# Attention in units of four heads: half-dimension tiles, scores over 32-row groups, new order of turns and evacuations

## The chip, the cores and the metric

The kernel runs on one core of a Trainium2 chip. The metric is the device time of one execution in microseconds (us). Names used below: PE is TensorE (PEld its weight loads), DVE is VectorE, ACT is ScalarE, POOL is GpSimd, SP is SyncE, which issues the DMAs.

## The reference

The whole reference is a chain of six residual blocks on x of shape (8, 256, 128) (in float32): a graph of small attentions, the attention below, the graph again, a mixture of experts, a Mamba block with an FFT branch, and the mixture again. The change touches only the second block:

```python
xn = (x - mu) / sqrt(var + 1e-5) * ln_gamma + ln_beta        # on _layernorm(x)
q, k, v = split(xn @ w_qkv)                                   # 16 heads of 64, 8 batches of 256 tokens
rotate(t) = concat([t1 * cos - t2 * sin, t2 * cos + t1 * sin])   # t1, t2: halves (32) of a head's 64 dimensions
scores = einsum('bhid,bhjd->bhij', rotate(q), rotate(k)) * 64 ** -0.5
out = einsum('bhij,bhjd->bhid', softmax(scores), v)
x = x + out.reshape(b, n, 1024) @ w_out + b_out
```

## The kernel before

The program is a row of phases with a barrier of all engines between them. In the attention phase (`attn_phase`) the unit of work is one pair of heads of one batch: 8 batches times 8 pairs are 64 units. All operands are float32; a float32 matmul appears in the trace as two MATMUL and two LDWEIGHTS instructions, a transpose as one of each.

`attn_schedule` runs one step per unit with four units in flight: f is projected, m (one behind) gets scores and exponentials, t (two behind) is normalized, turned and multiplied with v, u (three behind) goes through the output projection. Each engine has its own queue in program order, and counters (semaphores) tie them.

- TensorE: four projections of 256 columns (L796: q and k in a plain form, and q and k with the halves of each head swapped), v (L805), scores (L815: four matmuls of 256 columns; the keys lie in `km` with zeros in the other head's rows, so that each contracts over all 128 rows), eight transposes of the probabilities (L825), the output projection (L833, accumulated over the eight pairs of a batch in one bank), the context (L842, two column groups of 64).
- VectorE: reciprocal of the row sums (L856), normalization of the probabilities (L859, four instructions), the products with cos and sin (L868, one 512-column instruction for plain and one for swapped), row maximum (L873, one instruction over 1024 columns), its scaling (L875), the sums for k (L883), and once per batch the addition to x (L888).
- GpSimd: the sum for q (L911), a copy of the batch's tokens (L907).
- ScalarE: evacuation of v (L921), of the transposes (L926), four exponentials with row sums (L930), evacuation of the context (L935).

Seven banks of PSUM are in use: `plain`, `swapped`, two for scores, two for transposes (`tp`), one for v and context (`vc`), and `op`. The phase begins with five DMAs (L783, L784), all of which TensorE waits for.

Of the kernel before, what the change touches and what calls it, by code (L numbers as in the profile page):

```python
# [715 lines left out]
PAIRS = HA // 2  # L716
# [3 lines left out]
class Unit:  # L720


    def __init__(self, b, p):
        self.b, self.p, self.n = b, p, b * PAIRS + p


def attn_schedule(engine, step):

    def units(b, p, first=False):
        out = []  # L730
        for back in range(4):
            if p >= back:
                out.append(Unit(b, p - back))
            else:
                out.append(None if first else Unit(b - 1, p - back + PAIRS))
        return out

    for p in range(PAIRS):
        step(*units(0, p, first=True))
    with engine.Fori(1, B) as b:  # L740
        for p in range(PAIRS):
            step(*units(b, p))
    for late in range(1, 4):
        step(*([None] * late + [Unit(B - 1, PAIRS - 1 - i) for i in range(4 - late)]))


def attn_phase(k):

    nc, d = k.nc, k.d
    with ExitStack() as ctx:  # L750
        wqk = k.sb("at_wqk", [P, 4, HA * DA], ctx)
        wv = k.sb("at_wv", [P, HA * DA], ctx)
        wo = k.sb("at_wo", [P, PAIRS, D], ctx)
        rope = k.sb("at_rope", [P, 2, N], ctx)
        bo = k.sb("at_bo", [P, D], ctx)
        xb = k.sb("at_xb", [P, N], ctx)
        rot = k.sb("at_rot", [P, 2, 2, N], ctx)
        q = k.sb("at_q", [P, 2, N], ctx)
        km = k.sb("at_km", [P, 2, 2, N], ctx)
        v = k.sb("at_v", [P, VBUFS, 2, 2, DA], ctx)  # L760
        mx = k.sb("at_mx", [P, 2, 4], ctx)
        nmx = k.sb("at_nmx", [P, 2, 4], ctx)
        rsum = k.sb("at_rsum", [P, 2, 4], ctx)
        rinv = k.sb("at_rinv", [P, 2, 4], ctx)
        pr = k.sb("at_pr", [P, 2, 4, N], ctx)
        pt = k.sb("at_pt", [P, 2, 2, N], ctx)
        cx = k.sb("at_cx", [P, N], ctx)
        plain = k.psum("at_plain", [P, 2, N], ctx)
        swapped = k.psum("at_swapped", [P, 2, N], ctx)
        sc = k.psum("at_sc", [P, 4, N], ctx)  # L770
        tp = k.psum("at_tp", [P, 2, 2, N], ctx)
        vc = k.psum("at_vc", [P, 2, N], ctx)
        op = k.psum("at_op", [P, 512], ctx)
        names = ["loaded", "zeroed", "bias", "xb_sb", "proj_ps", "v_ps", "v_sb", "rot_sb", "q_sb", "km_sb", "sc_ps", "mx_sb", "nmx_sb",
# [3 lines left out]
        loads = [(wqk, "wqk"), (wv, "wv1"), (wo, "wout"), (rope, "rope")]  # L778

# [6 lines left out]
        @block.tensor  # L786
        def _(pe):
            def step(f, m, t, u):
                if f:

                    if not isinstance(f.n, int) or f.n:
                        pe.wait_ge(s["rot_sb"], f.n)
                    xs = k.xT[:, bass.ds(f.b * N, N)] if not isinstance(f.b, int) else k.xT[:, f.b * N:(f.b + 1) * N]
                    for i in range(4):
                        bank = plain if i < 2 else swapped
                        last = nc.tensor.matmul(bank[:, i % 2, :], wqk[:, i, f.p * P:(f.p + 1) * P], xs, start=True, stop=True)  # L796
                    last.then_inc(s["proj_ps"], 1)
                if f:
                    pe.wait_ge(s["xb_sb"], f.b + 1)
                    if u:  # L800
                        pe.wait_ge(s["cx_sb"], u.n + 1)
                    elif f.n:
                        pe.wait_ge(s["v_sb"], f.n)
                    for half in range(2):
                        last = nc.tensor.matmul(vc[:, 0, half * P:(half + 1) * P], xb[:, half * P:(half + 1) * P],  # L805
                                                wv[:, f.p * P:(f.p + 1) * P], start=True, stop=True)
                    last.then_inc(s["v_ps"], 1)
                if m:
                    pe.wait_ge(s["q_sb"], m.n + 1)
                    pe.wait_ge(s["km_sb"], m.n + 1)  # L810
                    if not isinstance(m.n, int) or m.n:
                        pe.wait_ge(s["pr_sb"], m.n)
                    for h in range(2):
                        for qh in range(2):
                            last = nc.tensor.matmul(sc[:, 2 * h + qh, :], q[:, m.p % 2, qh * P:(qh + 1) * P],  # L815
                                                    km[:, m.p % 2, h, :], start=True, stop=True)
                    last.then_inc(s["sc_ps"], 1)
                if t:
                    pe.wait_ge(s["pn_sb"], t.n + 1)
                    if not isinstance(t.n, int) or t.n:  # L820
                        pe.wait_ge(s["pt_sb"], 2 * t.n)
                    for h in range(2):
                        for qh in range(2):
                            for kh in range(2):
                                last = nc.tensor.transpose(tp[:, h, kh, qh * P:(qh + 1) * P],  # L825
                                                           pr[:, t.p % 2, 2 * h + qh, kh * P:(kh + 1) * P], k.ident[:, :])
                        last.then_inc(s["tp_ps"], 1)
                if u:
                    pe.wait_ge(s["cx_sb"], u.n + 1)
                    if u.p == 0 and (not isinstance(u.b, int) or u.b):  # L830
                        pe.wait_ge(s["x_sb"], u.b)
                    for half in range(2):
                        last = nc.tensor.matmul(op[:, half * P:(half + 1) * P], cx[:, half * P:(half + 1) * P], wo[:, u.p, :],  # L833
                                                start=u.p == 0 and half == 0, stop=u.p == PAIRS - 1, skip_group_check=True)
                    last.then_inc(s["op_ps"], 1)
                if t:
                    pe.wait_ge(s["pt_sb"], 2 * t.n + 2)
                    if f:
                        pe.wait_ge(s["v_sb"], f.n + 1)
                    for kh in range(2):  # L840
                        for h in range(2):
                            last = nc.tensor.matmul(vc[h * DA:(h + 1) * DA, 1, :], v[:, t.p % VBUFS, kh, h, :],  # L842
                                                    pt[:, h, kh, :], start=kh == 0, stop=kh == 1, tile_position=(0, h * DA))
                    last.then_inc(s["cx_ps"], 1)

            pe.wait_ge(s["loaded"], 16 * (len(loads) + 1))
            pe.wait_ge(s["zeroed"], 1)
            attn_schedule(pe, step)

        @block.vector  # L850
        def _(dve):
            def step(f, m, t, u):
                if t:

                    dve.wait_ge(s["pr_sb"], t.n + 1)
                    nc.vector.reciprocal(rinv[:, t.p % 2, :], rsum[:, t.p % 2, :]).then_inc(s["rinv_sb"], 1)  # L856
                    dve.wait_ge(s["rinv_sb"], t.n + 1)
                    for i in range(4):
                        last = nc.vector.tensor_scalar(pr[:, t.p % 2, i, :], pr[:, t.p % 2, i, :], rinv[:, t.p % 2, i:i + 1],  # L859
                                                       None, ALU.mult)  # L860
                    last.then_inc(s["pn_sb"], 1)
                if f:
                    dve.wait_ge(s["proj_ps"], f.n + 1)
                    if not isinstance(f.n, int) or f.n:
                        dve.wait_ge(s["q_sb"], f.n)
                        dve.wait_ge(s["km_sb"], f.n)
                    for i, bank in enumerate((plain, swapped)):
                        last = nc.vector.tensor_tensor(rot[:, i, :, :], bank[:, :, :],  # L868
                                                       rope[:, i:i + 1, :].broadcast_to([P, 2, N]), ALU.mult)
                    last.then_inc(s["rot_sb"], 1)  # L870
                if m:
                    dve.wait_ge(s["sc_ps"], m.n + 1)
                    nc.vector.tensor_reduce(mx[:, m.p % 2, :], sc[:, :, :], AX.X, ALU.max).then_inc(s["mx_sb"], 1)  # L873
                    dve.wait_ge(s["mx_sb"], m.n + 1)
                    nc.vector.tensor_scalar(nmx[:, m.p % 2, :], mx[:, m.p % 2, :], -(float(DA) ** -0.5), None, ALU.mult)\  # L875
                        .then_inc(s["nmx_sb"], 1)
                if f:
                    dve.wait_ge(s["rot_sb"], f.n + 1)
                    if not isinstance(f.n, int) or f.n >= 2:
                        dve.wait_ge(s["sc_ps"], f.n - 1)  # L880
# [972 lines left out]
```

## Time and profile before

| | us |
|---|---|
| median of three runs | 2776.11 (2773.88 to 2781.83) |
| the profiled execution's own time | 2771.16 |
| its span | 2769.3 |
| TensorE busy in the span | 2219.1 (80%) |
| VectorE, ScalarE, GpSimd busy | 1956.6, 1330.9, 812.3 |
| attention: first DMA issue, first matmul, end of the last addition to x | 608.3, 619.6, 1069.3 |

Busy time of a matmul includes its way through the array, so that consecutive ones overlap in the records; the pace is read from the starts of successive groups. "PEclk" is the granted clock of TensorE as a share of 2.4 GHz. A row of the order of time gives start, duration, engine, line, operation, output and inputs, and in brackets the idle time of that engine before it and who ended it.

### The profile page before, as it was taken

Reading aid. Unit: us, or ns where it says so; the run is one execution under the profiler, and the core shown is the slowest. Engines: PE = TensorE matmul, PEld = TensorE weight load, DVE = VectorE, ACT = ScalarE, POOL = GpSimd, SP = SyncE. Lnnn points to the kernel's source line nnn. Section 1 sums busy time; section 2 is a strip of 40 time slices with the busy share of each in tenths; the row PEclk is TensorE's granted clock in tenths of the full one; section 3 lists DMA queues with packets and bytes.
Section 4 is the critical chain, followed back from the end, with each engine's and each line's share of the span. In section 5 each row is a group of like instructions: output and inputs, shape, how many; then the busy total and the mean of one; then the engine's idle time right before and its main releaser. Section 6 shows DMA issues by size and latency. Waiting matters only on the chain. (4 is left out here: it accounts for less than half of the span.)

```text
span 2769.3 us, 41693 instructions
## 1 busy us (share of the span) xinstructions
PE 2219.1 (80%) x14388; PEld 1629.2 (59%) x14388; DVE 1956.6 (71%) x3310; ACT 1330.9 (48%) x2702; POOL 812.3 (29%) x1144
## 2 busy tenths in 40 slices
PE   2799999919999994799999946486877878878858
PEld 2466666617777773466666624274665655756634
DVE  4566666566666665566666554489899898998964
ACT  0466666615555552466666613345445445364422
POOL 0544444201111110544444202023323223233323
PEclk7899999959999997799999968698989989999969
DMA  1555555310000000555555300200000000000000
GB/s 62 144 132 136 134 138 133 79 52 1 1 0 0 0 0 0 145 133 136 135 137 132 78 14 12 116 0 0 1 1 1 1 0 0 0 0 1 1 12 15
DMA packets 147427, 144.31 MB, mean 52 GB/s; under 512 B 14401, under 2 KB 107201, under 8 KB 146497
## 3 DMA queue, kind: packets, MB, share of 16 engines
q1 hardware_dynamic: 147264, 142.23, 19.3%
q8 instruction: 92, 1.51, 0.2%
q14 instruction: 71, 0.57, 0.1%
HBM read 93.95 MB, written 38.80 MB: 48 GB/s over the span
## 5 line engine op out<-in xcount | busy, mean ns | idle before, releaser
L559 DVE TENSOR_REDUCE sb_f_mx<-ps_f_s 128x2 f32<-128x512 f32 x768 | 505.3, 688 | 315.8 <-PE ps_f_s L347 315.0
L500 ACT ACTIVATE sb_f_pt<-ps_f_t 128x1024 f32<-128x1024 f32 x384 | 391.7, 1021 | 90.3 <-PE ps_f_t L360 90.1
L1707 POOL TENSOR_TENSOR sb_mb_h<-sb_mb_h 128x1024 f32<-128x1024 f32 x64 | 157.7, 2464 | 656.5 <-DVE sb_mb_h L1601 656.5
L347 PE MATMUL ps_f_s<-sb_f_stack 96*128 96x256 bf16 x1536 | 287.4, 279 | 39.3 <-DMA sb_f_stack<-f_scr 22.1
L1595 DVE TENSOR_TENSOR_SCAN sb_mb_h<-sb_mb_da,sb_mb_h 128x1024 f32<-128x1024 f32 x128 | 310.5, 2466 | 2.4 <-ACT sb_mb_da L1466 0.3
L1336 PE MATMUL ps_mb_f<-sb_mb_fc,sb_mb_cw 128*128 128x256 f32 x1280 | 308.5, 404 | 0.0
L1336 PEld LDWEIGHTS ps_mb_f<-sb_mb_fc,sb_mb_cw 128*128 128x128 f32 x1280 | 260.2, 206 | 41.4
L1466 ACT ACTIVATE sb_mb_da<-sb_mb_dl,sb_mb_an 128x255 f32<-128x255 f32 x512 | 211.4, 496 | 70.2 <-DVE sb_mb_h L1595 65.7
L360 PE MATMUL ps_f_t<-sb_f_stack 128*128 128x256 bf16 x1536 | 233.0, 274 | 2.9 <-DMA sb_f_stack<-sb_f_mrow 2.8
L347 PEld LDWEIGHTS ps_f_s<-sb_f_stack 96*128 96x128 bf16 x1536 | 141.1, 99 | 91.2 <-DVE sb_f_mx L559 45.3
L619 POOL CAST sb_f_parts<-sb_f_qf 128x512 bf16<-128x512 f32 x96 | 58.5, 609 | 447.9 <-ACT sb_f_qf L527 447.9
L414 PE MATMUL ps_f_a<-sb_f_pt,sb_f_v 128*32 128x256 f32 x3072 | 185.7, 382 | 0.0
L360 PEld LDWEIGHTS ps_f_t<-sb_f_stack 128*128 128x128 bf16 x1536 | 141.1, 97 | 61.2 <-issue 38.7
L911 POOL TENSOR_TENSOR sb_at_q<-sb_at_rot 128x256 f32<-128x256 f32 x64 | 46.6, 728 | 394.1 <-DVE sb_at_rot L868 394.1
L1367 PE MATMUL ps_mb_c<-sb_mb_bc,sb_mb_sel 128*128 128x256 bf16 x256 | 46.1, 311 | 142.8 <-DVE sb_mb_h L1601 142.7
L1601 DVE TENSOR_TENSOR sb_mb_h<-sb_mb_h,ps_mb_c 128x1024 f32<-128x1024 f32 x128 | 150.6, 1218 | 2.2
L1587 DVE TENSOR_TENSOR sb_mb_h<-ps_mb_b,sb_mb_dx 128x1024 f32<-128x1024 f32 x128 | 150.3, 1216 | 0.7
L511 ACT ACTIVATE sb_f_cs<-ps_f_a 128x512 f32<-128x512 f32 x96 | 57.4, 597 | 186.7 <-PE ps_f_a L414 186.7
L414 PEld LDWEIGHTS ps_f_a<-sb_f_pt,sb_f_v 128*32 128x32 f32 x3072 | 90.1, 109 | 81.0 <-issue 31.6
L926 ACT ACTIVATE sb_at_pt<-ps_at_tp 128x512 f32<-128x512 f32 x128 | 69.6, 595 | 115.9 <-PE ps_at_tp L825 115.9
L815 PE MATMUL ps_at_sc<-sb_at_km,sb_at_q 128*128 128x256 f32 x512 | 121.3, 380 | 2.2 <-ACT sb_at_pr L930 2.2
L132 PE MATMUL ps_n_tp<-sb_ident,sb_n_y 128*128 128x128 f32 x96 | 24.5, 426 | 118.4 <-DVE sb_n_y L124 118.4
(242 smaller groups left out, 4571.7 us busy)
## 6 DMA issues: line engine op xcount, KB each, us to landing
f_scr<-sb_f_parts SPq DMA_DIRECT2D x96, 384.0 KB, 2.7
sb_f_stack<-f_scr SPq DMA_DIRECT2D x192, 192.0 KB, 3.1
sb_f_stack<-f_scr SPq DMA_DIRECT2D x192, 128.0 KB, 3.1
sb_f_stack<-f_scr SPq DMA_DIRECT2D x192, 64.0 KB, 3.4
sb_f_stack<-sb_f_mrow SPq DMA_DIRECT2D x96, 96.0 KB
sb_mb_cw<-in_cw SPq DMA_DIRECT2D x1, 5120.0 KB, 18.5
sb_at_wqk<-in_wqk SPq DMA_DIRECT2D x1, 2048.0 KB, 7.9
sb_m_w<-in_w SPq DMA_DIRECT2D x6, 256.0 KB, 3.2
```

The costliest lines, as they stand in the source:

```text
L347: last = nc.tensor.matmul(s_bank[j % 2][:, h, :], stack[0:ROWS, a.n % STACKS, 0, g * GROUP + pair * 2 + h, half * P:(half + 1) * P], stack ...
L360: last = nc.tensor.matmul(t_bank[i % 2][:, h, :], stack[:, e.n % STACKS, 1, g * GROUP + h, half * P:(half + 1) * P], stack[:, e.n % STACKS ...
L414: last = nc.tensor.matmul(act_bank[h * SLOT:(h + 1) * SLOT, g * N:(g + 1) * N], v[:, u.two, half, g * GROUP + h, :], pt[:, u.two, g, half, ...
L500: nc.scalar.activation(pt[:, e.two, g, half, :, :], t_bank[i % 2][:, :, :], ACT.Exp).then_inc(s["pt_sb"], 1)
L559: nc.vector.tensor_reduce(mx[:, a.two, half, head:head + 2], s_bank[j % 2][:, :, :], AX.X, ALU.max)\
L815: last = nc.tensor.matmul(sc[:, 2 * h + qh, :], q[:, m.p % 2, qh * P:(qh + 1) * P], km[:, m.p % 2, h, :], start=True, stop=True)
L1336: last = nc.tensor.matmul(f_bank[(1 + oc // 2) % 2][:, (oc % 2) * N:(oc % 2 + 1) * N], cw[:, ic, tap, oc * P:(oc + 1) * P], fc[:, ic, tap: ...
L1466: last = nc.scalar.activation(da[:, un % 2, c, i, 1:N], dl[:, m.parity, r, c, 1:N], ACT.Exp, scale=an[:, r, c, n:n + 1])
L1587: last = nc.vector.tensor_tensor(hb[:, c, :, :], b_bank[:, :, :], dx[:, m.parity, r, c:c + 1, :].broadcast_to([P, SG, N]), ALU.mult)
L1595: last = nc.vector.tensor_tensor_scan(flat, da[:, un % 2, c, :, :].rearrange("p i n -> p (i n)"), flat, 0.0, ALU.mult, ALU.add)
L1601: last = nc.vector.tensor_tensor(hb[:, c, :, :], hb[:, c, :, :], c_bank[:, :, :], ALU.mult)
L1707: nc.gpsimd.tensor_tensor(hb[:, :, 0:2, :], hb[:, :, 0:2, :], hb[:, :, 2:4, :], ALU.add)\
```

## The change

The unit becomes four heads of one batch (32 units, 36 steps written out one after another). q and k are projected as half-dimension tiles: four heads times 32 dimensions fill the 128 rows, first halves in one tile and second halves in another, so the swapped projections, `km`, its zeros and the copy `xb` are gone. VectorE multiplies each tile pair with cos and with sin (`rotate`), GpSimd does the two additions (one a subtraction) of q and the two of k. The scores of a head are two accumulated matmuls over its 32 rows, with `tile_position` giving the row group; the four heads write to four banks. Softmax lags two steps behind the projection, the transposes three, the output projection four. The output projection of a unit is written to half of the bank `vc`, and VectorE adds it to x once per unit. Transposes have two banks and come in two portions of two heads; evacuations, exponentials and normalizations are interleaved in halves.

```diff
+QUADS = HA // 4
+UNITS_A = B * QUADS
+SOFT_LAG, TURN_LAG, PROJ_LAG = 2, 3, 4
...
+        sc = [k.psum(f"at_sc{h}", [P, 2, N], ctx) for h in range(4)]
+        tp = [k.psum(f"at_tp{i}", [P, 2, N], ctx) for i in range(2)]
+        proj = k.psum("at_proj", [P, 2, N], ctx)
         vc = k.psum("at_vc", [P, 2, N], ctx)
...
+            def project(f, which):
+                if f.n or which:
+                    pe.wait_ge(s["rope_sb"], 2 * f.n + which)
+                for half in range(2):
+                    last = nc.tensor.matmul(proj[:, half, :], wqk[:, 2 * which + half, f.p, :], k.xT[:, f.b * N:(f.b + 1) * N],
+                                            start=True, stop=True)
+                last.then_inc(s["proj_ps"], 1)
+            def values(f, o):
+                if o:
+                    pe.wait_ge(s["x_sb"], o.n + 1)
...
+            def scores(m):
+                pe.wait_ge(s["rot_sb"], 4 * m.n + 4)
+                if m.n:
+                    pe.wait_ge(s["pr_sb"], 4 * m.n)
+                for qh in range(2):
+                    for half in range(2):
+                        for h in range(4):
+                            rows = slice(h * HALF, (h + 1) * HALF)
+                            last = nc.tensor.matmul(sc[h][:, qh, :], rot[rows, m.two, 0, half, qh * P:(qh + 1) * P],
+                                                    rot[rows, m.two, 1, half, :], start=half == 0, stop=half == 1,
+                                                    tile_position=(h * HALF, 0))
+                last.then_inc(s["sc_ps"], 1)
...
+            def add(o):
+                dve.wait_ge(s["op_ps"], o.n + 1)
...
+                nc.vector.tensor_tensor(xs, xs, vc[:, 0, :].rearrange("p (t d) -> p t d", t=2), ALU.add)\
+                    .then_inc(s["x_sb"], 1)
...
+        @block.gpsimd
...
+            def rotate(f, which):
+                pool.wait_ge(s["rope_sb"], 2 * f.n + which + 1)
...
+                nc.gpsimd.tensor_tensor(rot[:, f.two, which, 0, :], turned[:, which, 0, 0, :], turned[:, which, 1, 1, :],
+                                        ALU.subtract).then_inc(s["rot_sb"], 1)
+                nc.gpsimd.tensor_tensor(rot[:, f.two, which, 1, :], turned[:, which, 0, 1, :], turned[:, which, 1, 0, :],
+                                        ALU.add).then_inc(s["rot_sb"], 1)
```

With f = step, m = step - 2, t = step - 3 and o = step - 4, each engine's calls in a step are, in this order:

- TensorE: `scores(m)`, `turn(t, 0)`, `turn(t, 1)`, `project(f, 0)` (q), `turn(t, 2)`, `turn(t, 3)`, `project_out(o)`, `values(f, o)`, `project(f, 1)` (k), `context(t)`
- VectorE: `row_max(m, 0)`, `row_max(m, 1)`, `rotate(f, 0)`, `invert(m, 0)`, `normalize(m, 0)`, `add(o)`, `rotate(f, 1)`, `invert(m, 1)`, `normalize(m, 1)`
- ScalarE: `evacuate(t, 0)`, `evacuate(t, 1)`, `exponent(m, 0)`, `exponent(m, 1)`, `evacuate(t, 2)`, `evacuate(t, 3)`, v of f, `exponent(m, 2)`, `exponent(m, 3)`, `context(t)`
- GpSimd: `rotate(f, 0)`, `rotate(f, 1)`

The bodies that are not quoted carry the instructions of before at new sizes: `turn` is four transposes of one head, `context` eight matmuls in two column groups, `project_out` four matmuls of 128 columns, `project` and `values` two of 256; VectorE's `rotate` two products of 512 columns, `row_max` two reductions of 512 columns and one scaling, `normalize` four instructions of 256 columns; `evacuate` one copy of 512 columns, `exponent` two exponentials with row sums. `project_out(o)` waits for ScalarE's copy of the context, made in the step before.

## Rows read from the trace of the kernel before

**Rows 1.** Busy time by stretch: length, PE, PEld, DVE, ACT, POOL, clock, DMA.

```profile
608.30:619.60 11.30, 0.00 (x0) 0.00 (x0) 0.91 (x2) 0.00 (x0) 0.40 (x1) 0.55 0.81 307
...
634.20:1060.10 425.90, 402.16 (x2478) 329.61 (x2476) 293.10 (x691) 225.13 (x745) 47.26 (x69) 1.00 0.00 0
```

**Rows 2.** Order of time, one step of attention, with the batch's addition.

```profile
746.23 0.42 DVE L888 TENSOR_TENSOR sb_x<-sb_x,ps_at_op 128x256 f32 x1
...
748.94 1.89 PE L815 MATMUL ps_at_sc<-sb_at_km,sb_at_q 128*128 128x256 f32 x8
...
750.07 0.72 POOL L911 TENSOR_TENSOR sb_at_q<-sb_at_rot 128x256 f32<-128x256 f32 x1 [6.14 <-DVE sb_at_rot L868]
...
750.67 1.04 PE L825 MATMUL ps_at_tp<-sb_ident,sb_at_pr 128*128 128x128 f32 x8
750.87 1.23 DVE L873 TENSOR_REDUCE sb_at_mx<-ps_at_sc 128x4 f32<-128x1024 f32 x1 [0.88 <-PE ps_at_sc L815]
751.31 1.09 ACT L926 ACTIVATE sb_at_pt<-ps_at_tp 128x512 f32<-128x512 f32 x2 [1.78 <-PE ps_at_tp L825]
...
752.13 0.17 DVE L875 TENSOR_SCALAR sb_at_nmx<-sb_at_mx 128x4 f32<-128x4 f32 x1
...
752.34 0.47 ACT L930 ACTIVATE sb_at_pr<-ps_at_sc,sb_at_nmx 128x256 f32<-128x256 f32 x1
...
752.52 1.08 PE L842 MATMUL ps_at_vc<-sb_at_pt,sb_at_v 128*64 128x256 f32 x8 [0.37 <-ACT sb_at_pt L926]
...
753.54 1.13 PE L796 MATMUL ps_at_plain<-sb_xT,sb_at_wqk 128*128 x4
...
754.15 0.40 ACT L935 ACTIVATE sb_at_cx<-ps_at_vc 128x256 f32<-128x256 f32 x1
...
754.30 0.18 DVE L856 RECIPROCAL sb_at_rinv<-sb_at_rsum 128x4 f32<-128x4 f32 x1 [1.24 <-ACT sb_at_pr L930]
754.50 1.03 PE L796 MATMUL ps_at_swapped<-sb_xT,sb_at_wqk 128*128 x4
754.51 1.14 DVE L859 TENSOR_SCALAR sb_at_pr<-sb_at_pr,sb_at_rinv 128x256 f32<-128x256 f32 x4
...
755.37 0.61 PE L805 MATMUL ps_at_vc<-sb_at_wv,sb_at_xb 128*128 128x128 f32 x4
755.57 0.69 DVE L868 TENSOR_TENSOR sb_at_rot<-ps_at_plain,sb_at_rope 128x512 f32<-128x512 f32 x1
...
755.81 1.89 PE L815 MATMUL ps_at_sc<-sb_at_km,sb_at_q 128*128 128x256 f32 x8
...
756.18 0.68 DVE L868 TENSOR_TENSOR sb_at_rot<-ps_at_swapped,sb_at_rope 128x512 f32<-128x512 f32 x1
```

**Rows 3.** Order of time, first graph phase: four column groups, and two reductions.

```profile
301.54 1.93 PE L414 MATMUL ps_f_a<-sb_f_pt,sb_f_v 128*32 128x256 f32 x32
...
303.40 0.61 PE L360 MATMUL ps_f_t<-sb_f_stack 128*128 128x256 bf16 x4
...
306.17 1.28 DVE L559 TENSOR_REDUCE sb_f_mx<-ps_f_s 128x2 f32<-128x512 f32 x2
```

**Rows 4.** Order of time: VectorE beside GpSimd, in attention's first step and in Mamba.

```profile
624.78 1.29 DVE L883 TENSOR_TENSOR sb_at_km<-sb_at_rot 64x256 f32<-64x256 f32 x2
...
624.83 0.96 POOL L911 TENSOR_TENSOR sb_at_q<-sb_at_rot 128x256 f32<-128x256 f32 x1 [14.88 <-DVE sb_at_rot L868]
...
1901.71 1.27 POOL L1710 TENSOR_TENSOR sb_mb_h<-sb_mb_h 128x512 f32<-128x512 f32 x1
1901.89 1.51 DVE L1631 TENSOR_SCALAR sb_mb_vv<-sb_mb_vv,sb_mb_zo 128x256 f32<-128x256 f32 x2
```

**Rows 5.** After idle time of TensorE: one row of time, two stretches as in rows 1.

```profile
1063.48 1.97 PE L825 MATMUL ps_at_tp<-sb_ident,sb_at_pr 128*128 128x128 f32 x8 [2.18 <-DVE sb_at_pr L859]
...
1063.40:1066.80 3.40, 3.32 (x16) 2.90 (x18) 0.03 (x1) 1.20 (x2) 0.00 (x0) 0.51 0.00 0
...
2002.10:2005.50 3.40, 3.40 (x5) 1.33 (x4) 3.37 (x4) 3.05 (x5) 0.69 (x1) 0.51 0.00 0
```

More of the change, by code:

```diff
@@ L715, with __init__, attn_unit @@
 HA, DA = 16, 64
-PAIRS = HA // 2
+QUADS = HA // 4
+HALF = DA // 2
+UNITS_A = B * QUADS
+SOFT_LAG, TURN_LAG, PROJ_LAG = 2, 3, 4
 VBUFS = 4
 class Unit:
[L723 to L744, printed above, removed]
+    def __init__(self, n):
+        self.n = n
+        self.b, self.p = divmod(n, QUADS)
+        self.two = n % 2
+def attn_unit(step, lag):
+    return Unit(step - lag) if 0 <= step - lag < UNITS_A else None
 def attn_phase(k):
@@ L778, in attn_phase @@
         loads = [(wqk, "wqk"), (wv, "wv1"), (wo, "wout"), (rope, "rope")]
+        steps = range(UNITS_A + PROJ_LAG)
+        scale = float(DA) ** -0.5
         @block.sync
@@ L787, in _ @@
         def _(pe):
-            def step(f, m, t, u):
-                if f:
[L791 to L839, printed above, removed]
@@ new lines, in turn @@
+            def turn(t, h):
+                pe.wait_ge(s["pn_sb"], 2 * t.n + h // 2 + 1)
+                if t.n or h >= 2:
+                    pe.wait_ge(s["pt_sb"], 4 * t.n + h - 1)
+                for qh in range(2):
+                    for kh in range(2):
+                        last = nc.tensor.transpose(tp[h % 2][:, kh, qh * P:(qh + 1) * P],
+                                                   pr[:, t.two, 2 * h + qh, kh * P:(kh + 1) * P], k.ident[:, :])
+                last.then_inc(s["tp_ps"], 1)
@@ L840, in step, with context @@
+            def context(t):
+                f = attn_unit(t.n, -TURN_LAG)
+                o = attn_unit(t.n, 1)
+                pe.wait_ge(s["pt_sb"], 4 * t.n + 4)
+                if f:
+                    pe.wait_ge(s["v_sb"], f.n + 1)
+                elif o:
+                    pe.wait_ge(s["x_sb"], o.n + 1)
+                for pair in range(2):
                     for kh in range(2):
                         for h in range(2):
-                            last = nc.tensor.matmul(vc[h * DA:(h + 1) * DA, 1, :], v[:, t.p % VBUFS, kh, h, :],
-                                                    pt[:, h, kh, :], start=kh == 0, stop=kh == 1, tile_position=(0, h * DA))
@@ new lines, in context, with project_out @@
+                last.then_inc(s["cx_ps"], 1)
+            def project_out(o):
+                pe.wait_ge(s["cx_sb"], o.n + 1)
+                for half in range(2):
+                    for pair in range(2):
+                        last = nc.tensor.matmul(vc[:, 0, half * P:(half + 1) * P], cx[:, o.two, pair, half * P:(half + 1) * P],
+                                                wo[:, 2 * o.p + pair, :], start=pair == 0, stop=pair == 1)
+                last.then_inc(s["op_ps"], 1)
+            pe.wait_ge(s["loaded"], 16 * (len(loads) + 1))
@@ new lines, in _ @@
+            for step in steps:
+                f, m = attn_unit(step, 0), attn_unit(step, SOFT_LAG)
+                t, o = attn_unit(step, TURN_LAG), attn_unit(step, PROJ_LAG)
+                if m:
+                    scores(m)
+                if t:
+                    turn(t, 0)
+                    turn(t, 1)
+                if f:
+                    project(f, 0)
+                if t:
+                    turn(t, 2)
+                    turn(t, 3)
+                if o:
+                    project_out(o)
+                if f:
+                    values(f, o)
+                    project(f, 1)
+                if t:
+                    context(t)
@@ L850, in _ @@
         @block.vector
         def _(dve):
[L852 to L871, printed above, removed]
-                    dve.wait_ge(s["sc_ps"], m.n + 1)
[L873 to L880, printed above, removed]
-                    for h in range(2):
-                        rows = slice(h * DA, (h + 1) * DA)
-                        last = nc.vector.tensor_tensor(km[rows, f.p % 2, h, :], rot[rows, 0, 1, :], rot[rows, 1, 1, :], ALU.add)
-                    last.then_inc(s["km_sb"], 1)
-                if u and u.p == PAIRS - 1:
-                    dve.wait_ge(s["op_ps"], u.n + 1)
-                    xs = k.x[:, bass.ds(u.b * 2, 2), :] if not isinstance(u.b, int) else k.x[:, 2 * u.b:2 * u.b + 2, :]
-                    nc.vector.tensor_tensor(xs, xs, op[:, 0:N].rearrange("p (t d) -> p t d", t=2), ALU.add)\
-                        .then_inc(s["x_sb"], 1)
@@ new lines, in row_max @@
+            def row_max(m, pair):
+                if pair == 0:
+                    dve.wait_ge(s["sc_ps"], m.n + 1)
+                for h in (2 * pair, 2 * pair + 1):
+                    last = nc.vector.tensor_reduce(mx[:, m.two, 2 * h:2 * h + 2], sc[h][:, :, :], AX.X, ALU.max)
+                last.then_inc(s["mx_sb"], 1)
+                dve.wait_ge(s["mx_sb"], 2 * m.n + pair + 1)
+                nc.vector.tensor_scalar(nmx[:, m.two, 4 * pair:4 * pair + 4], mx[:, m.two, 4 * pair:4 * pair + 4], -scale,
+                                        None, ALU.mult).then_inc(s["nmx_sb"], 1)
@@ new lines, in invert, with normalize @@
+            def invert(m, pair):
+                dve.wait_ge(s["pr_sb"], 4 * m.n + 2 * pair + 2)
+                nc.vector.reciprocal(rinv[:, m.two, 4 * pair:4 * pair + 4], rsum[:, m.two, 4 * pair:4 * pair + 4])\
+                    .then_inc(s["rinv_sb"], 1)
+            def normalize(m, pair):
+                dve.wait_ge(s["rinv_sb"], 2 * m.n + pair + 1)
+                for i in range(4 * pair, 4 * pair + 4):
+                    last = nc.vector.tensor_scalar(pr[:, m.two, i, :], pr[:, m.two, i, :], rinv[:, m.two, i:i + 1],
+                                                   None, ALU.mult)
+                last.then_inc(s["pn_sb"], 1)
@@ L896, in _ @@
             dve.wait_ge(s["bias"], 1)
-            attn_schedule(dve, step)
+            for step in steps:
+                f, m, o = attn_unit(step, 0), attn_unit(step, SOFT_LAG), attn_unit(step, PROJ_LAG)
+                if m:
+                    row_max(m, 0)
+                    row_max(m, 1)
+                if f:
+                    rotate(f, 0)
+                if m:
+                    invert(m, 0)
+                    normalize(m, 0)
+                if o:
+                    add(o)
+                if f:
+                    rotate(f, 1)
+                if m:
+                    invert(m, 1)
+                    normalize(m, 1)
@@ L916, in _, with evacuate @@
+            for step in steps:
+                f = attn_unit(step, 0)
+                if f:
+                    rotate(f, 0)
+                    rotate(f, 1)
         @block.scalar
         def _(act):
-            def step(f, m, t, u):
+            def evacuate(t, h):
+                act.wait_ge(s["tp_ps"], 4 * t.n + h + 1)
+                if t.n and h == 0:
+                    act.wait_ge(s["cx_ps"], t.n)
+                nc.scalar.activation(pt[:, h, :, :], tp[h % 2][:, :, :], ACT.Copy).then_inc(s["pt_sb"], 1)
@@ new lines, in context, with exponent @@
+            def context(o):
+                act.wait_ge(s["cx_ps"], o.n + 1)
+                if o.n >= 2:
+                    act.wait_ge(s["op_ps"], o.n - 1)
+                nc.scalar.activation(cx[:, o.two, :, :], vc[:, :, :], ACT.Copy).then_inc(s["cx_sb"], 1)
+            def exponent(m, h):
+                act.wait_ge(s["nmx_sb"], 2 * m.n + h // 2 + 1)
+                if m.n >= 2 and h == 0:
+                    act.wait_ge(s["tp_ps"], 4 * (m.n - 1))
+                for i in (2 * h, 2 * h + 1):
+                    last = nc.scalar.activation(pr[:, m.two, i, :], sc[h][:, i % 2, :], ACT.Exp, scale=scale,
+                                                bias=nmx[:, m.two, i:i + 1], accum_out=rsum[:, m.two, i:i + 1])
+                last.then_inc(s["pr_sb"], 1)
@@ L940 @@
+                if m:
+                    exponent(m, 2)
+                    exponent(m, 3)
+                if t:
+                    context(t)
 EXPERTS, HID = 8, 64
```

113 lines of the change are left out of this document (55 added, 58 removed).

## Prediction, made before the changed kernel was run

> **What bounds the kernel now.** I read the busy time by stretch first, since the change touches one phase, and then the order of time of one step. From 634 to 1060 us TensorE is busy for 402 of 425.9 us at a granted clock of 1.00, VectorE for 293, ScalarE for 225, GpSimd for 47 [rows 1]: attention is bound by TensorE. A step takes 755.81 - 748.94 = 6.87 us [rows 2], in which TensorE has one stall of 0.37 us (the context waits for ScalarE's copy of the transposes). Four heads therefore cost 13.74 us now, and the phase 449.7 us from its first matmul to its last addition. Ahead of it stand 11.3 us in which the five DMAs run at 307 GB/s and TensorE does nothing [rows 1]. The reader is to see that a float32 matmul of 256 columns has a pace of 0.43 us (projections: 754.50 to 755.37 for two), one of 128 columns 0.22 (755.37 to 755.81 for two), a transpose 0.11 (1.04 for eight less the 0.17 that the last takes to come out), and that two column groups run side by side: the four context matmuls and the change of array layout behind them take 753.54 - 752.52 = 1.02, so 0.86 and 0.15 [rows 2].
>
> **TensorE's work for four heads.** Projections: 8 matmuls become 4, so 3.46 becomes 1.73. v stays 0.87, transposes 1.74, output projection 0.87, context 1.71 + 0.12 for the change of layout. Scores: 8 matmuls of 0.43 (3.46) become 16, of which four, on four row groups, may run side by side: 4 x 0.43 = 1.71, with 0.13 + 0.15 at its ends. No row of before has row groups. The nearest are four column groups: 32 instructions in 303.40 - 301.54 = 1.86 [rows 3], 1.71 of it at full speed, so four at a time exactly. The bounds are 1.71 and, one at a time, 6.84; I take 1.71. Sum: 9.03 us against 13.74. Were TensorE still the bound, 32 units would save 150 us.
>
> The Trainium skill, in "TensorE: Matmul & The Clock Gate", Measured speedup vs the span model, gives 3.07x instead of 4x for four row groups of 32. By it the scores would take 2.2 us, half a microsecond more a unit, some 16 us in all as an estimate from that page; no run so far shows it.
>
> **VectorE's work.** Reductions over 512 columns have a pace of 0.60 (two in 1.28, one alone 0.69 [rows 3]); two, the wait for the result and the scaling make 1.41, and twice that 2.82. The two products 1.20 per call (pace 0.61 [rows 2]). Reciprocal to first normalization 0.21; four normalizations 1.06 until the next can begin (754.51 to 755.57). The addition to x 0.42, now once per unit instead of once per eight pairs. Sum 2.82 + 2.40 + 0.42 + 2.12 + 0.42 = 8.2 us, less than TensorE's. ScalarE has six copies of 512 columns at a pace of 0.54 (two in 1.09) and eight exponentials at 0.45 (752.34 to 754.15 for four): 6.9. GpSimd has four additions of 0.72: 2.9. None of these is a bound by its sum.
>
> **The wait that the change adds.** `vc` holds the output projection of unit o, which VectorE must add to x before `values` may write there, and then v, and then the context. `values`, `project(f, 1)` and `context` are queued behind that wait on TensorE, and behind the context the next scores. On VectorE the addition stands behind all of `row_max`, `rotate(f, 0)` and the first normalizations. So the step becomes a loop through both engines. From the start of the scores: VectorE sees them after 1.93 (750.87 - 748.94) + 0.13 = 2.06; row maxima 2.82 (4.88); products 1.20 (6.08); reciprocal 0.21 (6.29); normalizations 1.06; addition 0.42; back to TensorE 0.10; v and k 1.73; context 1.83. That is 11.43. TensorE is finished with `project_out` at 5.47, and stands still until about 7.9.
>
> **GpSimd beside the normalizations.** GpSimd's first addition for q is released by the same products, 0.08 behind them, so it begins at 6.24, just ahead of the first normalization at 6.29. The rows show that the two exclude each other: a POOL addition runs from 1901.71 to 1902.98, two normalizations of the same 256 columns, asked for at 1901.89, last 1.51 instead of 0.61 and end 0.42 behind it; and q's own addition took 0.96 instead of 0.72 beside VectorE's sums of two tiles from the SBUF, of which the second did not end before it [rows 2, 4]. In attention before, GpSimd ran while VectorE waited for scores, so nothing of this was paid. Now: addition 6.24 to 6.96, normalization to 7.13, second addition to 7.72 (0.59 behind), then three more normalizations until 8.42: 0.98 later than alone. The bounds are 0 and 1.44 (both additions in full); I take 0.98. The loop is 12.41 us. ScalarE is level with it: v's copy at 9.94 (behind the wait), two pairs of exponentials until 12.34, and the next scores wait for them. TensorE stands still from 5.47 to 8.85, 3.4 us in each step, and VectorE's second half, with the same collision, ends 1.9 us into the next step, just ahead of the scores' 2.06.
>
> **Filling and emptying.** The same walk, from the first matmul with VectorE's 2.3 us for the bias ahead of it, puts the first scores 9.4 us behind the first matmul, the next 8 and 11 later, and the last addition 17 behind the last scores but none; of 403 us, 28 full steps are 347.5 and the four at each end together 55.5 (45 to 65, as these steps wait in other places). The unrolled program has nothing to pay for: the graph phases are written out too.
>
> **The clock.** TensorE's clock is 1.00 throughout attention before. At the phase's end TensorE waited 2.18 us, and the same eight transposes then took 1.97 instead of 1.04, at a granted clock of 0.51 (1.2 GHz) over the next 3.4 us; another stretch of 3.4 us at 0.51 lies in Mamba [rows 2, 5]. The new step has a stall longer than that 2.18, every time, and what comes behind the stall (v, k, context: 3.4 us of matmuls) lies on the loop. One fall costs 3.4 us at half speed, so 1.7. The bounds are no fall and one per step; as the stall is 1.2 us longer than the one in the row, I take one per step: 32 x 1.7 = 54 us.
>
> **The load.** `wqk` shrinks by 1.05 MB: at 307 GB/s 3.4 us less ahead of the first matmul (bounds 0 and 4).
>
> **The sum.** 403 + 54 = 457 for the phase against 449.7: +7.5; load -3.4; the other phases as before. The profiled execution's own 2771.2 becomes 2775.2; the median of the runs lies 4.9 above it, so about **2780 us**. What TensorE no longer does (150 us) is lost again to the loop through VectorE (12.41 - 9.03 = 3.4 us x 32 = 108) and to the clock (54). Its own range is 2757 to 2805: the stall by 0.3 and the addition by 0.1 us each way, and falls in two steps of three (-18).
>
> **Rivals.**
> - *The clock holds.* The stall is longer than any in attention before, but TensorE is busy for 9 of 12.4 us, and one row at the end of the phase is thin evidence. Then the phase takes 403: 2776 - 47 - 3 = 2726 (2712 to 2740). Against it: two stretches at 0.51 behind low activity, none of them far from this one. 0.13.
> - *GpSimd doesn't get in the way*, since the normalizations win the race for the port at 6.29 or the additions are ended sooner. Then the loop is 11.4 to 11.9, the stall 2.4, and a fall comes in half of the steps or fewer: 372 to 388 plus 32 x 0.8, about 405: 2728 (2700 to 2745). Against it: three rows of collision. 0.15.
> - *The row groups don't run four at a time* (the side that is clearly slower). Each of the 32 weight loads of a unit's scores is 128 columns wide, where the column groups' were 32. If loads of 128 columns come one behind another at the 0.11 that four matmuls of 128 columns or eight transposes keep up at best, the scores take 3.5 and everything behind them is 1.8 later: the loop 14.2, the phase 455 with the clock at 1.00 and about 470 with a few falls: 2793 (2785 to 2815). Each 0.25 us on the scores is 8 us in 32 steps, so this decides from scores of about 2.0 us on. One group at a time, 6.84, would make it 17.5 a step, 565 to 580: about 2900. For it: TensorE has never been seen so here; against it: the column groups, which lose nothing. 0.15 for the first and 0.04 for the second.
>
> The skill has a rule for the third: in "TensorE: Matmul & The Clock Gate", LDWEIGHTS, the load of 32 rows by 128 columns takes as long as that of 128 rows. No trace here shows a load of 32 rows; the rows with 32 columns can't tell.
>
> **Chances.** My case 0.53, the clock holds 0.13, no collision 0.15, slow row groups 0.15 and 0.04. A measurement of this kernel tells 0.3%, 8 us, from no change. My case is 25% below 2768, 35% within, 40% above; the second and third are faster, the rest nearly all slower: faster 0.13 + 0.28 = 0.41, same 0.20, slower 0.39. The range is 2718 to 2820; it leaves out the serial row groups and the ends of the second and third.
>
> **What would show it.** Right: matmuls of the scores about 1.9 from first to last; TensorE idle some 3.4 us ahead of `values`, ended by VectorE's addition; `normalize(m, 0)` about 2.0 instead of 1.1; a granted clock near 0.85 over the phase; steps of about 14 us. Wrong: a clock of 1.00 (then 2726), normalizations of 1.1 beside GpSimd, or scores that take 3.5.

## The result, and the profile after

| us | before | changed |
|---|---|---|
| median of 14 runs each | 2775.78 (2770.82 to 2781.83) | 2786.03 (2783.11 to 2792.11) |
| the profiled execution's span | 2769.3 | 2784.9 |
| load of attention: first DMA issue to first matmul | 11.3 | 8.5 |
| attention: first matmul to end of the last addition to x | 449.7 | 462.9 |

The ratio is 1.0038, with a 95% interval of 1.0031 to 1.0046: slower by 0.38%, 10.3 us. The forecast was 2780. The phase is 13.2 us longer and the load 2.8 shorter, so 10.4 in all, which is the difference of the medians (10.25); the other 5 us between the two spans lie in phases that are the same in both.

The stretches of the changed kernel that answer to [rows 1], then short ones behind TensorE's stall, as in [rows 5] (length, busy time of PE, PEld, DVE, ACT, POOL, granted clock, DMA share, GB/s):

```profile
608.50:617.10 8.60, 0.01 (x1) 0.01 (x1) 0.03 (x1) 0.00 (x0) 0.00 (x0) 0.50 0.73 282
...
634.20:1060.10 425.90, 335.91 (x2488) 251.18 (x2486) 298.18 (x631) 205.55 (x659) 86.95 (x120) 0.86 0.00 1
...
799.90:803.30 3.40, 3.18 (x8) 2.50 (x8) 0.17 (x1) 1.07 (x4) 0.00 (x0) 0.50 0.00 0
...
814.30:817.70 3.40, 3.40 (x8) 2.47 (x8) 0.00 (x0) 1.33 (x5) 0.00 (x0) 0.50 0.00 0
...
813.60:820.40 6.80, 6.15 (x20) 4.01 (x22) 2.89 (x8) 2.42 (x9) 0.96 (x2) 0.50 0.00 0
```

TensorE has lost its place as the bound: 336 of 425.9 us busy instead of 402, and part of that at half speed (mean clock 0.86, where it was 1.00). VectorE's busy time has hardly moved (298 against 293), although it now does less: its instructions have become longer.

One step in order of time, which answers to [rows 2]:

```profile
805.50 1.61 PEld L805 LDWEIGHTS ps_at_sc<-sb_at_rot 32*128 32x128 f32 x32 [0.38 <-issue]
805.50 2.01 PE L805 MATMUL ps_at_sc<-sb_at_rot 32*128 32x256 f32 x32
...
807.58 1.29 DVE L886 TENSOR_REDUCE sb_at_mx<-ps_at_sc 128x2 f32<-128x512 f32 x2 [0.35 <-PE ps_at_sc L805]
...
810.11 1.06 PE L843 MATMUL ps_at_vc<-sb_at_wo,sb_at_cx 128*128 128x128 f32 x8
...
811.58 0.17 DVE L895 RECIPROCAL sb_at_rinv<-sb_at_rsum 128x4 f32<-128x4 f32 x1
811.74 0.72 POOL L945 TENSOR_TENSOR sb_at_rot<-sb_at_turned 128x256 f32<-128x256 f32 x1 [5.19 <-DVE sb_at_turned L877]
811.78 2.09 DVE L902 TENSOR_SCALAR sb_at_pr<-sb_at_pr,sb_at_rinv 128x256 f32<-128x256 f32 x4
812.42 0.77 POOL L947 TENSOR_TENSOR sb_at_rot<-sb_at_turned 128x256 f32<-128x256 f32 x1
813.79 0.41 DVE L912 TENSOR_TENSOR sb_x<-sb_x,ps_at_vc 128x256 f32<-128x256 f32 x1
...
814.25 2.08 PE L792 MATMUL ps_at_vc<-sb_at_wv,sb_xT 128*128 128x256 f32 x4 [3.09 <-DVE sb_x L912]
...
816.12 1.91 PE L781 MATMUL ps_at_proj<-sb_xT,sb_at_wqk 128*128 128x256 f32 x4
```

The chain reads from the top: scores, row maxima, products, reciprocal; GpSimd's addition begins 0.04 us ahead of the first normalization, and the four normalizations take 2.09; then the addition to x, and only then v, after 3.09 us in which TensorE stands still. v and k, 1.13 and 1.03 long at full speed (below), take 2.08 and 1.91: half speed, as the row 814.30:817.70 has it. This fall of the clock is one of the long ones, from 813.6 to 820.4; the one of the step before lasts 3.4 us, from 799.9 to 803.3.

The waits from 640 to 1040 us (total, times, longest) and three groups of instructions there (count, busy time, mean in ns, idle before):

```profile
POOL sb_at_rot L945 <- DVE sb_at_turned L877: 318.5, 56, 6.4
ACT sb_at_v L998 <- PE ps_at_vc L792: 109.5, 27, 4.4
DVE sb_at_turned L877 <- PE ps_at_proj L781: 95.2, 27, 3.9
...
PE ps_at_vc L792 <- DVE sb_x L912: 83.8, 27, 3.5
```

```profile
L902 DVE TENSOR_SCALAR sb_at_pr<-sb_at_pr,sb_at_rinv 128x256 f32<-128x256 f32 x224 | 117.0, 581 | 2.0
...
L805 PE MATMUL ps_at_sc<-sb_at_rot 32*128 32x256 f32 x896 | 56.3, 387 | 0.0
...
L805 PEld LDWEIGHTS ps_at_sc<-sb_at_rot 32*128 32x128 f32 x896 | 43.2, 184 | 12.6 <-issue 5.8 <-POOL sb_at_rot L945 2.7 <-POOL sb_at_rot L947 2.3
```

TensorE's only large wait is the one for the addition to x: 27 times 3.1 us. VectorE and ScalarE then wait for what TensorE does late, and GpSimd's 318 us of waiting cost nothing. A normalization takes 581 ns on average; the same line of before stands here for comparison, in the same stretch of its trace:

```profile
L859 DVE TENSOR_SCALAR sb_at_pr<-sb_at_pr,sb_at_rinv 128x256 f32<-128x256 f32 x232 | 66.2, 350 | 2.1
```

Steps (from v to v) come in fours: three of 14.1 to 14.2 us, with a fall of 3.4 us, and one of 15.5, with a fall of 6.8; the 27 steps from 655.61 to 1046.36 have a mean of 14.47, and six of them are long.

### The profile page after: what moved, and what is told of

It reads as the page before. It is cut to its first block and busy times, and to the rows that moved or that the text cites. A ratio compares the mean times of both kernels' runs of the same rounds, so it can differ in the third digit from the quotient of the medians.

```text
span 2784.9 us, 41434 instructions
## 1 busy us (share of the span) xinstructions
PE 2166.4 (78%) x14516; PEld 1560.0 (56%) x14516; DVE 1968.4 (71%) x3269; ACT 1319.0 (47%) x2638; POOL 853.8 (31%) x1200
## 5 line engine op out<-in xcount | busy, mean ns | idle before, releaser
L945 POOL TENSOR_TENSOR sb_at_rot<-sb_at_turned 128x256 f32<-128x256 f32 x64 | 46.4, 724 | 428.4 <-DVE sb_at_turned L877 428.4
L877 DVE TENSOR_TENSOR sb_at_turned<-ps_at_proj,sb_at_rope 128x512 f32<-128x512 f32 x128 | 82.4, 685 | 103.6 <-PE ps_at_proj L781 103.5
L902 DVE TENSOR_SCALAR sb_at_pr<-sb_at_pr,sb_at_rinv 128x256 f32<-128x256 f32 x256 | 130.0, 567 | 2.3
L792 PE MATMUL ps_at_vc<-sb_at_wv,sb_xT 128*128 128x256 f32 x128 | 55.1, 574 | 86.9 <-DVE sb_x L912 86.9
```

What stands on the lines that cost most here:

```text
L902: last = nc.vector.tensor_scalar(pr[:, m.two, i, :], pr[:, m.two, i, :], rinv[:, m.two, i:i + 1], None, ALU.mult)
```

## The experiments

My theory had three parts: the place of VectorE's addition to x makes a loop through both engines; GpSimd's additions lengthen the normalizations in it by 0.98 us; the stall that is left lets TensorE's clock fall once a step. Experiments 1 and 2 take away the second and the third alone, 3 and 5 the first, 6 and 7 the first together with the second, and 4 and 8 put a price on the order of the row groups. Medians are beside before's 2773.79 (1 to 4) and 2774.27 (5 to 8).

**1. GpSimd behind the normalizations.** Its additions wait for the normalizations of the same half.

```diff
@@ GpSimd, rotate(f, which), if f.n >= 2
+                    pool.wait_ge(s["pn_sb"], 2 * (f.n - 2) + which + 1)
```

> GpSimd's additions wait for the normalization of the unit two behind, so that they no longer run beside it; nothing else is changed. Theory (the step is a loop through VectorE, lengthened by the collision and by clock falls): the four normalizations ahead of the addition to x take 1.14 us instead of 2.09, TensorE's stall ahead of v shrinks from 3.1 to about 2.1, falls of the clock become rarer, the phase goes from 463 to between 375 (no fall) and 415 us (a fall in every second step), the whole to about 2730 us (2700 to 2740). Rival A (the loop does not run through the normalizations): no change, 2786. Rival B (the clock falls because of the new kinds of matmul and not because of the stall): the clock stays near 0.86, the phase at 463 - 31 = 432, the whole 2755.

Measured: 2743.56 us, ratio 0.9882 (0.9865 to 0.9898). Order of time:

```profile
798.86 1.14 DVE L902 TENSOR_SCALAR sb_at_pr<-sb_at_pr,sb_at_rinv 128x256 f32<-128x256 f32 x4
799.91 0.42 DVE L912 TENSOR_TENSOR sb_x<-sb_x,ps_at_vc 128x256 f32<-128x256 f32 x1
800.13 0.73 POOL L946 TENSOR_TENSOR sb_at_rot<-sb_at_turned 128x256 f32<-128x256 f32 x1 [6.28 <-DVE sb_at_pr L902]
800.38 1.13 PE L792 MATMUL ps_at_vc<-sb_at_wv,sb_xT 128*128 128x256 f32 x4 [2.14 <-DVE sb_x L912]
...
811.99 1.82 PE L792 MATMUL ps_at_vc<-sb_at_wv,sb_xT 128*128 128x256 f32 x4 [2.14 <-DVE sb_x L912]
```

The normalizations are back at 1.14 and the stall is 2.14, 0.95 shorter: the collision was real and lay wholly on the loop. What was expected wrongly is the clock. The time is 3.6 us above the top of the expected range, because falls did not become rare: of the 27 steps from 657.95 to 1005.79 (v to v) 21 take 13.25 us and six 11.6, and the mean clock from 634 to 1010 us is 0.90. One fall, 3.4 us long, therefore costs 1.6 us here (13.25 - 11.61). GpSimd's later additions cost nothing: no scores wait for them in these steps.

**2. TensorE kept busy in the stall.** Four matmuls behind the output projection, into a transpose bank that nobody reads; the output is unchanged.

```diff
@@ TensorE, between project_out(o) and values(f, o)
+                if f and t and o:
+                    pe.wait_ge(s["pt_sb"], 4 * t.n + 4)
+                    for i in range(4):
+                        nc.tensor.matmul(tp[0][:, i % 2, :], wqk[:, 0, 0, :], k.xT[:, 0:N], start=True, stop=True)
```

> Between the output projection and v, where TensorE stands still, it computes four matmuls of 256 columns (1.7 us) whose result nobody reads, once the last evacuation of the transposes is done; the loop through VectorE is the same. Theory: the stall is cut into two of about 1 and 0.5 us, the clock stays at 1.00, steps become 12.4 us as walked for an undisturbed clock, the phase 403 to 410, the whole about 2730 us. Rival B (the falls come from the kind of matmuls): clock 0.86 as before, 2786 or more. Rival C (falls matter little, since the loop waits for VectorE anyway): clock 1.00 but no gain, 2780 to 2786.

Measured: 2729.49 us, ratio 0.9832 (0.9816 to 0.9849). A kernel with 448 more instructions on TensorE (16 in each of 28 steps) is 56 us faster than the change (2786.03). One step, and the stretch from 634 to 1010 us:

```profile
800.23 2.01 PE L805 MATMUL ps_at_sc<-sb_at_rot 32*128 32x256 f32 x32
...
806.52 2.09 DVE L906 TENSOR_SCALAR sb_at_pr<-sb_at_pr,sb_at_rinv 128x256 f32<-128x256 f32 x4
806.80 1.99 PE L866 MATMUL ps_at_tp<-sb_xT,sb_at_wqk 128*128 128x256 f32 x8 [0.91 <-ACT sb_at_pt L967]
808.53 0.41 DVE L916 TENSOR_TENSOR sb_x<-sb_x,ps_at_vc 128x256 f32<-128x256 f32 x1
808.99 1.13 PE L792 MATMUL ps_at_vc<-sb_at_wv,sb_xT 128*128 128x256 f32 x4 [0.19 <-DVE sb_x L916]
809.96 1.03 PE L781 MATMUL ps_at_proj<-sb_xT,sb_at_wqk 128*128 128x256 f32 x4
...
812.79 2.01 PE L805 MATMUL ps_at_sc<-sb_at_rot 32*128 32x256 f32 x32
```

```profile
634.00:1010.00 376.00, 337.39 (x2727) 260.50 (x2728) 293.50 (x639) 210.30 (x675) 87.57 (x120) 1.00 0.01 1
```

This is the loop without the clock: v still waits for the addition to x, the normalizations still take 2.09, but nothing in these steps runs at half speed, and every one is 12.56 us. The four matmuls end before the addition to x does (808.79 and 808.94), so they don't lengthen the loop. So the falls cost 14.47 - 12.56 = 1.91 us a step: 1.6 for a short one and 3.0 for a long one. That the clock holds with the same matmuls in every other place refutes the rival that their kind makes it fall. The run is also a ruler for the walk of the prediction, from the start of the scores: normalizations at 6.29 (forecast 6.29), addition to x at 8.30 (8.33), v at 8.76 (8.85), next scores at 12.56 (12.41).

**3. The addition to x ahead of the normalizations.**

```diff
@@ VectorE
+                if o:
+                    add(o)
                 ...invert(m, 0), normalize(m, 0)...
-                if o:
-                    add(o)
```

> VectorE's addition to x goes ahead of the first normalization instead of behind it; same work, same number of instructions. Theory: v can be written 2.1 us earlier, TensorE's stall falls from 3.1 to about 1 us, there are hardly any falls of the clock, a step takes about 10.2 us, the phase 338 to 345 us, the whole about 2665 us (2655 to 2690). Rival A (TensorE is held by something else, such as ScalarE's exponentials, which are level with the loop): at most the fall of the clock is gained, 2730 or more. Rival B (falls from the kind of matmul): 345 + 50, 2720.

Measured: 2668.71 us, ratio 0.9620 (0.9603 to 0.9637). Order of time:

```profile
801.31 2.01 PE L805 MATMUL ps_at_sc<-sb_at_rot 32*128 32x256 f32 x32
...
807.39 0.41 DVE L912 TENSOR_TENSOR sb_x<-sb_x,ps_at_vc 128x256 f32<-128x256 f32 x1
807.55 0.72 POOL L945 TENSOR_TENSOR sb_at_rot<-sb_at_turned 128x256 f32<-128x256 f32 x1 [5.18 <-DVE sb_at_turned L877]
...
807.86 1.13 PE L792 MATMUL ps_at_vc<-sb_at_wv,sb_xT 128*128 128x256 f32 x4 [0.88 <-DVE sb_x L912]
807.92 1.76 DVE L902 TENSOR_SCALAR sb_at_pr<-sb_at_pr,sb_at_rinv 128x256 f32<-128x256 f32 x4
...
811.66 2.01 PE L805 MATMUL ps_at_sc<-sb_at_rot 32*128 32x256 f32 x32
```

Moving one call ahead of two others takes the normalizations and their collision off the loop, the stall falls to 0.88, and with it the falls end (clock 0.99 from 634 to 960 us). The step is 10.35 and the phase 344.3. The change's own instructions, in this order, are 3.8% faster than the kernel before.

**4. Heads outermost in the scores.** The same 16 matmuls, four of one row group behind each other.

```diff
-                for qh in range(2):
-                    for half in range(2):
-                        for h in range(4):
+                for h in range(4):
+                    for qh in range(2):
+                        for half in range(2):
```

> The 16 matmuls of the scores in another order: all four of one head, then the next head, instead of the four heads in turn. Same work. If the four row groups run side by side only when neighbours in the queue are of different groups: scores 6.9 us instead of 2.0, 32 x 4.9 = 157 us more, about 2940 us. If TensorE's queue finds matmuls for an idle row group further back: 2.0 us and 2786. I hold the first for likelier, 2 to 1.

Measured, one run: 2872.45 us. In its order of time the scores are

```profile
809.04 4.91 PE L805 MATMUL ps_at_sc<-sb_at_rot 32*128 32x256 f32 x32
```

Neither 6.9 nor 2.0; 32 times the 2.9 us more is 93, and the kernel is 86 slower than the change. With the groups' matmuls bunched, TensorE overlaps only part of them. So running side by side depends on what stands next to what in the queue, and the change had the good order.

**5. The output projection right behind the scores,** and its addition to x between the two row maxima.

```diff
@@ TensorE
                 scores(m)
+                if o:
+                    project_out(o)
                 ...turn, project(f, 0), turn...
-                if o:
-                    project_out(o)
@@ VectorE
                     row_max(m, 0)
+                if o:
+                    add(o)
+                if m:
                     row_max(m, 1)
                 ...rotate(f, 0), invert(m, 0), normalize(m, 0)...
-                if o:
-                    add(o)
```

> TensorE issues the output projection right behind the scores, and VectorE adds it to x between the two row maxima of the first two heads. Theory (the price of the change is the place of that addition, which holds `vc`): the loop through VectorE is gone from v, k and the context; steps of about 10.1 us at a clock of 1.00, a phase of 342 us, and about 2665 us, level with the addition moved ahead of the normalizations alone. Rival (the collision with GpSimd still sets the step, as the normalizations stay 2.0): steps of 10.8 or more, and 2685.

Measured: 2662.35 us, ratio 0.9599 (0.9582 to 0.9616). Order of time:

```profile
810.03 1.29 DVE L877 TENSOR_TENSOR sb_at_turned<-ps_at_proj,sb_at_rope 128x512 f32<-128x512 f32 x2
811.24 0.17 DVE L895 RECIPROCAL sb_at_rinv<-sb_at_rsum 128x4 f32<-128x4 f32 x1
811.37 1.13 PE L781 MATMUL ps_at_proj<-sb_xT,sb_at_wqk 128*128 128x256 f32 x4 [0.37 <-DVE sb_at_turned L877]
811.40 0.73 POOL L946 TENSOR_TENSOR sb_at_rot<-sb_at_turned 128x256 f32<-128x256 f32 x1 [5.08 <-DVE sb_at_turned L877]
811.44 2.10 DVE L902 TENSOR_SCALAR sb_at_pr<-sb_at_pr,sb_at_rinv 128x256 f32<-128x256 f32 x4
811.72 0.65 ACT L999 ACTIVATE sb_at_v<-ps_at_vc 128x512 f32<-128x512 f32 x1
...
812.51 1.95 PE L833 MATMUL ps_at_vc<-sb_at_pt,sb_at_v 128*64 128x256 f32 x16
```

v no longer waits at all; the one stall left is k's, 0.37 us for the bank of the projections. Steps are 9.96 us, the phase 336.1 (expected 10.1 and 342). The normalizations are as slow as ever, 2.10, and the rival (steps of 10.8 or more) is refuted. But VectorE has hardly any slack left, since it is busy for 9.82 us of one step:

```profile
804.43:814.39 9.96, 9.58 (x86) 7.51 (x85) 9.82 (x22) 6.79 (x22) 2.93 (x4) 1.00 0.00 0
```

Whether the collision costs something here, only experiment 6 can tell.

**6. The same with GpSimd behind the normalizations** (the edits of 5 and 1 together).

> The same, and GpSimd's additions wait until the normalizations of the same half are done. Theory (the collision costs where VectorE is on the path): as VectorE has only 8.2 us of work and TensorE 9.0, GpSimd's lateness is worth little now, 0.2 to 0.3 us a step: steps of 9.8, about 2655. Rival (GpSimd's additions now come late for the scores): steps over 10.5 and 2680 or more, slower than without the wait.

Measured: 2657.18 us, ratio 0.9573 (0.9557 to 0.9589): the fastest, but its interval overlaps that of 5, so a gain by GpSimd's wait is not shown. The step is 9.96 as there (expected 9.8):

```profile
806.17 1.14 DVE L902 TENSOR_SCALAR sb_at_pr<-sb_at_pr,sb_at_rinv 128x256 f32<-128x256 f32 x4
...
806.74 0.65 ACT L1000 ACTIVATE sb_at_v<-ps_at_vc 128x512 f32<-128x512 f32 x1
...
807.53 1.95 PE L833 MATMUL ps_at_vc<-sb_at_pt,sb_at_v 128*64 128x256 f32 x16 [0.40 <-ACT sb_at_v L1000]
...
809.24 0.18 DVE L895 RECIPROCAL sb_at_rinv<-sb_at_rsum 128x4 f32<-128x4 f32 x1 [0.73 <-ACT sb_at_pr L980]
```

VectorE is busy for 8.19 us of a step now instead of 9.82, and nothing is gained. The context shows why: it begins 0.14 us behind the end of ScalarE's copy of v here (807.39), and in experiment 5 just as much (812.37). So the path through ScalarE set the step there too, k's stall and the collision lay beside it, and both cost nothing.

**7. The early addition with GpSimd behind the normalizations** (3 and 1 together).

> VectorE's addition to x ahead of the reciprocal and the normalizations, and GpSimd's additions behind the normalizations. Theory: the stall ahead of v (0.88 with the early addition alone) stays, as it ends with the addition to x, which neither GpSimd nor the normalizations precede now; the normalizations go back to 1.14. Steps 10.2, about 2660 (2652 to 2670). Rival: the additions, now later by about 1 us, hold the scores, and it is slower than the early addition alone (2668.7): 2680 or more.

Measured: 2667.56 us, ratio 0.9611 (0.9595 to 0.9627), beside 2668.71 without the wait: the same. The stall ahead of v is 0.88 as before it, the normalizations 1.14, the step 10.35. The rival (late additions hold the scores) is refuted, too.

**8. Two matmuls of one row group behind each other.**

```diff
                 for qh in range(2):
-                    for half in range(2):
-                        for h in range(4):
+                    for h in range(4):
+                        for half in range(2):
```

> The scores' 16 matmuls loop over the row half outermost, then the heads, and the dimension's halves innermost: always two matmuls of one row group behind each other, where with the heads outermost it was four (4.91 us), and in the change one (2.01). First theory (TensorE begins an instruction while about three ahead of it are unfinished, in their order; each change of row group then overlaps some 0.64 us, as 6.84 - 4.91 at three changes shows): seven changes, 11 times 0.213 = 2.35 us and its ends, 2.5; 2786 + 32 x 0.5 = about 2802. Second (never more than two row groups at a time unless each instruction changes the group): 3.4 us, about 2831.

Measured, one run: 2793.27 us, and

```profile
808.49 2.12 PE L805 MATMUL ps_at_sc<-sb_at_rot 32*128 32x256 f32 x32
```

2.12 us is nearer to the first theory's 2.5 than to the second's 3.4, but hits neither. Two matmuls of a group in a row are nearly free, four are not; what rule gives 2.01, 2.12 and 4.91 stays open.

## Why the prediction was right, and which terms were off

**TensorE's work for four heads: right where it decides.** The scores take 2.01 us from first to last, where the sum had 1.71 and 0.28 for their ends. Four row groups run four at a time: 32 weight loads of 184 ns each lie within 1.61 us, so their width of 128 columns doesn't make them wait for each other. Both "slow row groups" rivals are refuted by this row. The Trainium skill's 3.07x ("TensorE: Matmul & The Clock Gate", Measured speedup vs the span model) would have made them 2.2 us plus ends of 0.3, as an estimate from that page; the trace is at 2.01 with its ends and disagrees. The Trainium skill ("TensorE: Matmul & The Clock Gate", LDWEIGHTS) has a load of 32 rows as long as one of 128; the trace agrees for one load, 184 ns, beside a mean of 190 for the loads of 128 rows of the scores of before, in the same stretch (row below). The fault of the rival was to add the loads up one after another. The whole sum of 9.03 us bounds no run: the shortest steps, of experiments 5 and 6, are 9.96 us.

```profile
L815 PEld LDWEIGHTS ps_at_sc<-sb_at_km,sb_at_q 128*128 128x128 f32 x469 | 84.7, 190 | 9.1
```

**The wait that the change adds: right.** Every step has TensorE idle ahead of v, ended by VectorE's addition. Experiment 2 gives the loop without the clock, 12.56 us for a forecast of 12.41: the context takes 1.88 instead of 1.83, and ScalarE, which was level with it, has the rest: the context begins 0.16 us behind the end of its copy of v. The stall in row 814.25, behind which TensorE runs at half speed as behind that of [rows 5], was mis-sized, 3.09 for 3.4. The prediction had TensorE finished 5.47 us after the scores' start; by the rows above it is at 811.17, 5.67, and v begins 0.10 earlier than forecast.

**GpSimd beside the normalizations: right,** in size (2.09 instead of 1.14, so 0.95 for 0.98) and in consequence (experiment 1). The rival without a collision is refuted. The Trainium skill ("SBUF — State Buffer", Who interferes with whom) calls the pair of ports that the two engines share an exclusive lock. The trace agrees: of the four normalizations from 811.78 on, the first two take 0.83 and 0.81 us and each ends 0.15 behind one of GpSimd's additions, the other two take 0.34. All four are only 0.95 later than alone, where GpSimd's additions together run for 1.45 us, so that the first normalization gets in between the two.

**The clock: right in kind, and right in size by luck, as two errors cancel.** A fall like the assumed one, 3.4 us long, costs 1.6 us (14.19 - 12.56, and 13.25 - 11.61 in experiment 1), a little less than the 1.7 assumed. But in every fourth step it lasts 6.8 us and costs 3.0, which the prediction did not foresee, so the mean is 1.91. And it costs that in the 27 steps from 655.61 on, 51.6 us, where the prediction had all 32 pay; filling and emptying add only about 1. In all that is 52.7 us (462.9 less the 410.2 of experiment 2's phase) for 54. The rival "the clock holds" gave 2726, and experiment 2, which makes it hold, 2729.5. But what the second rival said of the clock, that a stall of 2.4 would have a fall in half of the steps or fewer, is refuted by experiment 1: 21 of 27 at 2.14.

**The sum: 6 us short.** Phase without falls in its steps 410.2 for 403: 28 steps at 0.15 more are 4.2, filling and emptying 3.0 more (the clock is at 0.50 from 1017.9 to 1021.3 in experiment 2's emptying, so a part of the 3.0 is a fall). The load shrank by 2.8 instead of 3.4, at 282 GB/s in place of the 307 assumed. With 1.3 less for the clock: 7.2 - 1.3 + 0.6 = 6.5, and 2780 + 6.5 is the measured median within half a microsecond. Each is smaller than what the walk could claim; but with the forecast's sum at +4, half the measurement's bound, they decide between "the same" and "slower". The prediction had the time and the mechanism, but not the sign: it gave "slower" 0.39 and "faster" 0.41.

## What to carry to other kernels

A new wait is priced by where it stands in both queues: here one addition of 0.41 us stood behind 2.2 us of reciprocal and normalizations that TensorE did not need yet; moving it up by two calls saved 117 us and turned 0.4% slower into 3.8% faster. Before a kernel is called bound by an engine, look at what the stall does to that engine's clock: filling it with matmuls for nobody gave 56 us back. And a collision of two engines costs only where the lengthened one is on the path that sets the step: 0.95 us a step in experiment 1, nothing between experiments 5 and 6. Remove the loop first; the collision may not be worth an edit.

## What the runs showed of the hardware that was not expected

- The order of matmuls on different row groups decides how far they overlap: 16 float32 matmuls of 256 columns (32 instructions) take 2.01 us when each is on another group than the one before, 2.12 with two of a group in a row, 4.91 with four in a row.
- With a stall of 2.14 us in a step that takes 11.6 without a fall, the clock still falls in 21 of 27 steps; one of 0.88 in 10.35 leaves it at 0.99. The pattern is regular: steps come in fours in the changed kernel (three of 14.1 to 14.2, one of 15.5), in experiment 1 every fourth or fifth step is free of the fall. Why, no run here shows.
